# Multi-level attention with a four-layer feed-forward: softmax sums inverted and spread by DMAs, and a new order of tasks

## The reference

```
qkv = x @ w_in.T + b_in
scores = q @ k.T / sqrt(16);  attn = softmax(scores);  out = attn @ v
outs[l] = out @ w_out.T + b_out
```

## Time and profile before

| | us |
|---|---|
| median of 3 runs (lowest, highest) | 3565.03 (3562.65, 3567.78) |
| profiled execution, its own time | 3567.79 |
| profiled execution, span | 3566.0 |
| TensorE matmul busy | 3373.3 (95%) |
| VectorE busy | 2532.4 (71%) |
| ScalarE busy | 2529.9 (71%) |
| POOL busy | 1044.3 (29%) |

### The profile page before, as it was taken

The page is one execution under the profiler, slowest core; times in us unless marked ns, Lnnn a source line. Parts: engine busy times, 40 slices in busy tenths (PEclk is TensorE's granted clock), DMA queues, the critical chain, the costliest instruction groups (busy, mean ns, idle before and its releaser), DMA issues. The chain is left out here.

```text
span 3566.0 us, 58276 instructions
## 1 busy us (share of the span) xinstructions
PE 3373.3 (95%) x20635; PEld 1393.0 (39%) x20635; DVE 2532.4 (71%) x4805; ACT 2529.9 (71%) x3266; POOL 1044.3 (29%) x1060
## 2 busy tenths in 40 slices
PE   6999999999999999999999989799999999999998
PEld 3333333333333333333333322244444444444444
DVE  5989988988998998998998989634333333433333
ACT  2899889889889889889889878644444444444443
POOL 3343543544454454453464342300000000000000
PEclk7999999999999999999999999999999999999999
DMA  5343433433333333343343332200000000000000
GB/s 184 109 143 112 126 89 100 129 93 98 113 100 102 111 115 95 109 121 92 109 124 90 113 94 81 81 1 19 19 13 13 13 13 13 16 22 13 13 13 13
DMA packets 237691, 269.82 MB, mean 76 GB/s; under 512 B 55876, under 2 KB 203460, under 8 KB 236768
## 3 DMA queue, kind: packets, MB, share of 16 engines
q1 hardware_dynamic: 228144, 257.10, 24.2%
q10 hardware_dynamic: 9216, 8.39, 0.7%
HBM read 159.75 MB, written 101.45 MB: 73 GB/s over the span
## 5 line engine op out<-in xcount | busy, mean ns | idle before, releaser
L1009 ACT ACTIVATE a_probs<-a_p_s,a_unit_now 128x1024 f32<-128x1024 f32 x1360 | 1440.4, 1113 | 169.1 <-PE a_p_s L1407 164.9
L1135 DVE TENSOR_REDUCE a_part_max<-a_p_r 128x1 f32<-128x512 f32 x2048 | 1289.7, 679 | 112.9 <-PE a_p_r L1420 107.6
L1420 PE MATMUL a_p_r<-a_k_st,a_q_st 48*128 48x512 f16 (+2 forms) x2944 | 862.2, 374 | 94.1 <-DVE a_part_max L1135 44.3
L1757 PE MATMUL p_h<-f_h_hi,f_w_hi 128*128 128x512 f16 x2048 | 777.8, 380 | 9.8 <-issue 9.8
L1757 PE MATMUL p_h<-f_h_lo,f_w_hi 128*128 128x512 f16 x2048 | 777.6, 380 | 0.0
L1468 PE MATMUL a_p_o<-a_probs,a_v_aug 128*17 128x512 f32 (+2 forms) x5888 | 724.0, 571 | 1.0 <-ACT a_raw L1019 0.2
L1407 PE MATMUL a_p_s<-a_q_st,a_k_st 50*128 50x512 f16 (+2 forms) x2944 | 646.0, 368 | 18.4 <-ACT a_probs L1009 15.6
L1420 PEld LDWEIGHTS a_p_r<-a_k_st,a_q_st 48*128 48x128 f16 x2944 | 217.4, 94 | 976.7 <-DVE a_part_max L1135 654.8
L1656 ACT ACTIVATE f_h_f<-p_h,f_sc_now 128x512 f32<-128x512 f32 x256 | 175.9, 687 | 524.8 <-PE p_h L1757 524.8
L1135 DVE TENSOR_REDUCE a_row_max<-a_p_r 128x1 f32<-128x512 f32 (+2 forms) x672 | 417.9, 679 | 33.7 <-PE a_p_r L1420 32.5
L1607 POOL TENSOR_TENSOR f_rstd<-f_var_eps,f_minus_half 128x1 f32<-128x1 f32 x64 | 35.5, 555 | 1222.5 <-DVE f_var_eps L1720 1222.5
(11 more groups left out here) (170 smaller groups left out, 4454.4 us busy)
## 6 DMA issues: line engine op xcount, KB each, us to landing
qk_scratch<-a_qk_room SPq DMA_DIRECT2D x288, 128.0 KB
a_q_st<-qk_scratch SPq DMA_DIRECT2D x240, 96.0 KB, 2.4
a_w_lo<-wqkv_inner SPq DMA_DIRECT2D x30, 768.0 KB, 5.6
a_a_lo<-a_attn SPq DMA_DIRECT2D x448, 32.0 KB, 2.0
a_k_st<-qk_scratch SPq DMA_DIRECT2D x64, 192.0 KB, 3.6
a_o_lo<-wo_inner SPq DMA_DIRECT2D x24, 512.0 KB, 3.6
a_qk_room<-wf SPq DMA_DIRECT2D x23, 512.0 KB, 3.8
a_k_st<-qk_scratch SPq DMA_DIRECT2D x112, 96.0 KB, 2.3
```

The lines of the kernel that those rows point to most:

```text
L1009: act.activation(probs[:, s % 2, 2 * p:2 * p + 2, :], p_s[:, 2 * p:2 * p + 2, :], ACT.Exp, scale=unit_now[:, lvl:lvl + 1]).then_inc(exp_do ...
L1135: dve.reduce_max(out, src, AX.X).then_inc(max_read.sem, 1)
L1420: ins = pe.matmul(p_a[:, r * size:(r + 1) * size], q_st[rows_of(j, ROWS), query_at:query_at + 128], k_st[rows_of(j, ROWS), key_at:key_at + ...
L1757: ins = pe.matmul(out, a, c, start=first and n == 0, stop=last and n == len(terms) - 1)
```

## The change

The kinds `turn` and the old `spread` leave VectorE. Three new kinds of SP come in, each one DMA a unit:

- `sums`: the four rows of sums of `raw` (4 partitions of 512 values) go to a new tile `sums`, 128 x 16, 32 partitions for each row.
- `rows`: after VectorE has inverted `sums` into `rec`, this brings `rec` back over the four rows of sums in `raw`.
- `spread`: each of these rows is copied from `raw` over the 32 partitions of its head in the `attn` tile. It first waits until `rows` has landed and until the ring's slot is free.

`invert` on VectorE now waits for `sums` to have landed, and for the `rows` of the unit two before. POOL's `attn` waits for `spread` to have landed. The code of the new kinds (`hold()` and `held` count up a semaphore that nobody waits for, between two waits):

```diff
+                        elif kind == "sums":
+                            sp.wait_ge(raw_done.sem, raw_done.value(it, n + 1))
+                            hold()
+                            rec_done.wait(sp, it, max(n - 1, 0))
+                            hold()
+                            sp.dma_start(sums[:, n % 2, :], raw[HD:128:32, n % 2, :]).then_inc(sums_in[n % 2].sem, 16)
+                        elif kind == "rows":
+                            sp.wait_ge(rec_done.sem, rec_done.value(it, n + 1))
+                            hold()
+                            sp.dma_start(raw[HD:128:32, n % 2, :], rec[:, n % 2, :]).then_inc(rows_in[n % 2].sem, 16)
+                        elif kind == "spread":
+                            rows_in[n % 2].wait(sp, it, n // 2 + 1)
+                            hold()
+                            packed[n % RING].wait(sp, it, PACKED[n - RING] if n >= RING else 0)
+                            hold()
+                            sp.dma_start(attn[:, n % RING, :], raw[HD:128:32, n % 2, :].unsqueeze(1).broadcast_to((HG, 32, W))).then_inc(spread_in[n % 2].sem, 16)
...
-                            pool.wait_ge(spread_done.sem, spread_done.value(it, 2 * n + 2))
+                            spread_in[n % 2].wait(pool, it, n // 2 + 1)
...
-                            dve.transpose(attn[:, u % RING, cols], raw[:, u % 2, cols]).then_inc(turned_done.sem, 1)
...
-                            dve.reciprocal(rec[:, n % 2, :], attn[:, n % RING, :].rearrange("p (c r) -> p c r", r=32)[:, :, HD]).then_inc(rec_done.sem, 1)
...
-                            dve.transpose(attn[:, u % RING, cols], rec[:, u % 2, part * W // 64:(part + 1) * W // 64].unsqueeze(2).broadcast_to((128, W // 64, 32)))\
...
+                            sums_in[n % 2].wait(dve, it, n // 2 + 1)
+                            dve.sem_inc(held.sem, 1)
+                            rows_in[n % 2].wait(dve, it, n // 2)
+                            dve.sem_inc(held.sem, 1)
+                            dve.reciprocal(rec[:, n % 2, :], sums[:, n % 2, :]).then_inc(rec_done.sem, 1)
```

All tables of places are new: `AT`, `OPEN`, `FIRST`, `LAST`, `HEAD` and the shifts. The last two weight chunks of the feed-forward get kinds of their own (`w3load`, `w3hi`, `w3lo`, `w3check`) with the same work. Of the tables, those that the text speaks of:

```diff
-MAX_TURN, SCORE_TURN, VALUE_TURN = (0.04, 0.06, 0.4, 0.55), (0.46, 0.55), 2.07
+MAX_TURN, SCORE_TURN, VALUE_TURN = (0.28, 0.31, 0.46, 0.47), (0.5, 0.65), 2.31
...
-    "sp": {"proj": 2.2, "neg": 1.6, "attn": 1.8, "finish": 1, "keep": 0.5},
+    "sp": {"proj": 1.58, "neg": 0.08, "attn": 2.77, "finish": 6.47, "keep": 0.21, "fstore": 2, "fout": 1, "rows": 0.62, "fetch": -6.21, "stack": -0.64, "spread": 0.94, "sums": -0.8},
...
-    "raw": (3.24, 5.08, 9.27, 13.29, 16.87, 21.29, 21.71, 30.29, 38.14, 46.3, 54.29, 61.79, 70.45, 78.28, 84.87,),
+    "raw": (3.77, 5.3, 9.3, 13.51, 17.44, 21.31, 22.86, 31.01, 38.34, 46.14, 54.34, 62.3, 70.48, 78.55, 85.5,),
-    "invert": (5.49, 9.38, 12.5, 13.78, 18.68, 21.82, 25.82, 32.81, 40.07, 48.94, 57.9, 63.07, 71.05, 79.13, 86.75,),
+    "invert": (5.39, 7.56, 12.71, 14.5, 19.78, 23.35, 25.87, 36.19, 40.35, 49.31, 56.14, 63.79, 73.01, 79.5, 86,),
+    "rows": (3.7, 7.65, 10.82, 14.18, 18.06, 23.28, 25.13, 35.09, 40.04, 46.63, 55.7, 61.86, 72.02, 80.81, 83.42,),
+    "spread": (4.87, 7.55, 12.98, 15, 19.55, 24.06, 25.13, 35.57, 40.8, 49.03, 55.55, 63.72, 75.91, 80.53, 84.59,),
+    "sums": (3.6, 6.6, 9.81, 13.95, 17.08, 22.11, 22.6, 32.48, 40.71, 47.12, 52.41, 62.6, 72.47, 78.6, 84.78,),
+    "neg": (-8.19, -3.41, -2.84, 1.12, 5.81, 9.43, 10.07, 18.54, 27.44, 34.62, 41.49, 50.15, 57.56, 65.85, 73.4,),
```

More of the change, by code:

```diff
@@ new lines @@
+    "unit": (0.6,),
+    "v": (-53.98, -31.12, -28.9, -10.53, 0.6, 2.64, 18.63, 20.55,),
+    "wcut": (-54.32, -36.47, -14.52, -6.85,),
+    "wload": (-90.83, -43.55, -19.17, -13.34,),
+    "x": (-99.01, -33.96,),
+    "xcopy": (-11.84, -4.09, 1.61, 7.69, 9.75, 14.62, 63.23, 23.4,),
+    "xcut": (-55.4, -9.03,),
+}
+FIRST = {"acut": 2, "attn": 5, "invert": 5, "max": 132, "neg": 8, "proj": 15, "raw": 5, "rows": 5, "score": 42, "span": 4, "spanned": 4, "spread": 5,
+        "stack": 9, "sums": 5, "unit": 1, "v": 8, "value": 19, "wcut": 4, "wload": 4, "x": 2, "xcut": 2}
@@ L341 @@
+    "pool": {"raw": -5.09, "invert": 2.49, "spread": -12.52, "attn": 4.17, "acut": -1.36, "fetch": -6.83, "sum": -7.83, "out": 0.08, "stats": 1.03,
+        "gather": -21.93, "finish": -1.23, "sums": 2, "rows": 4.33},
+    "sp": {"raw": 8.82, "invert": -1.22, "spread": 4.03, "attn": 4.22, "acut": -13.38, "fetch": -8.3, "sum": -7.97, "out": -1.95, "stats": 1.85,
+        "gather": 8.87, "finish": 3.71, "sums": 3.46, "rows": 1.82},
 }
```

198 lines of the change are left out of this document (85 added, 113 removed).

## The result

The changed kernel takes 3828.0 us, median of four runs (3824.3 to 3831.6); the kernel before, on the same chips, 3566.4 us (3562.7 to 3568.9). The ratio is 1.073, with an interval of 95% from 1.072 to 1.074: 262 us slower. I had forecast 3495 us, with a range of 3415 to 3567. The change goes the wrong way, and none of my rivals had its size either: the slowest of them, C, stood at 3613 us.

A forecast was written before the change was run, and what follows sets the result against it. VectorE was taken to pace the coarse part, with three engines holding each other in the fine part. Freed transposes -87, turns +10 and last batch +5 gave -72 us, hence 3495 us; range 3415 to 3567.

The forecast's parts named there:

- C: Rival: SP's order holds the queue at `rows` and `spread`, so scores start late at each unit; 3613 us, chance 0.12.
- Part 3: Three new DMAs a unit on SP: room for their issues, bytes hidden; taken 0, ends 0 and +6 us a batch.
- Part 4: Longer chain from raw copy to product, some 8 us: +10 us over seven batch turns, +5 in the last batch.
- The paragraph on four engines: New DMAs use 4 engines; 256 KB takes an estimated 2.4 us plus the fixed part, making the sum 14 us later.
- Part 1: Four transposes a unit leave VectorE: 168 us freed, gain 63 in coarse parts plus 24 in fine, 87 us.
- Rival A: ScalarE and TensorE take over at once; first part gives 5 a batch, second nothing: 3545 us, chance 0.18.
- Part 2: VectorE's reciprocal reads a packed tile and gets two waits: no difference taken, waits 0 to +1 us a batch.
- Part 5: New places in the order, within steps and at the opening: taken 0, trusted to 20 us either way.
- The sum: -87 + 10 + 5 = -72 us off the profiled 3567.8; median near 3494, said 3495.
- signs of being wrong: Score weight loads waiting for DMAs, reductions waiting behind a reciprocal, ScalarE above 95%, or a fine part short as the coarse.

## Why the prediction was wrong, step by step

The 262 us come apart by differences between neighbouring kernels: -29 (the division left out, old order), -22 (all the new places at once), +72 (the chain with a quick source, product free of it), +191 (the slow source), +49 (the product has to wait). That is 311 - 51, with rounding. The order in which they are taken matters little where two are on record: the source is worth 197 us when the product waits and 191 when it doesn't, the product's wait 42 us with the fast source (3630.9 - 3588.5) and 49 with the slow one.

**Step that failed first: parts 3 and 4, the copy's duration and its bytes.** I priced each new DMA at the 2.0 us of the packing, and wrote of the 31 MB "hidden". The write back bore it out, 1.4 to 2.8 us to the next issue, and so did the gather in half of the cases in which it was waited for (1.5 to 2.2 us to the reciprocal), but it went up to 8.7. The third copy, 32 times as large, took 6.4 to 8.7 us, where I had put 2 to 4.5 as the sign of being right. A bare chain of 8 us was 12.1 (raw copy's end at 1316.16 to product at 1328.26). Worse than the length was what I hadn't a term for: a copy that holds a quarter of the DMA engines for 5.3 us at every unit makes its neighbours late and their issues long, and against a fast source that alone is 191 us, though nobody's product waits for it. I looked at the DMA share (35 to 38%) and found room; it rose only to 0.47 and 0.38 in the two parts. A mean share says nothing of what a 4 KB copy meets that leaves right behind a slow one. I had read the one wait for `neg` in the earlier trace rows, 1.2 us, as a sign against trouble; it says only that these copies landed in time while nothing slow stood beside them.

**The paragraph on four engines.** The Trainium skill (DMA: Bandwidth & Descriptors, Why a DMA increments its semaphore by 16 and not by 1) had the count right: the view shows a quarter of the engines busy. My estimate of 2.4 us for the bytes, which rests on Where 436 GB/s comes from in the same page of the Trainium skill, fits the source in device memory, where a quarter of the engines moved 100 GB/s. Out of four partitions they moved 49, and with 16 engines it got no better. So even with that estimate the sum would have been 14 us later and on the wrong side.

**Part 1, VectorE's gain.** Mis-sized: 87 us with ends 35 and 168, measured 28.7 with the reciprocals gone too, under my lower end. As a mean the coarse part gave 3.0 us a batch, not 9, and the fine one 0.5, not 3. The last fine part gave 5.7, and at its end I had expected nothing. The work that went was less than I took as well: VectorE's busy row fell by 134.7 us in the changed kernel, 0.28 us a transpose, where I had generalised 0.35 from one pair in the earlier trace rows and foretold 168. I read 96% busy as "bound by VectorE" and took nearly all of what was freed. Rival A had this side right (its -35 is the nearest figure), though not the time.

**Part 2, waits of the reciprocal.** Taken 0, ends 0 to +1 us a batch. VectorE waited 119.2 us in all, 15 a batch. Its place is behind the raw copy's in the order, but raw copies came late and the gather left later still, as at the turn above: the reciprocal's turn had been due 5.65 us, of which the gather's own flight is 2.2. What waits for what is right as I named it, and the wait of VectorE for maxima went from 107.6 to 313.6 us; how much of it goes by way of the reciprocal no run divides.

**Part 3, SyncE.** 0.65, 0.61 and 0.55 us of issue, as taken; but I had not asked what they do to the issues behind them, up to 2.1 us for one DMA of 4 KB where 0.6 is the longest with the fast source. SP's holds for the chain are real, but the kernel with fewer of them took 4020 us. Rival C said "slower, by late hand-overs", decided from 0.6 us a unit; it was 311 / 120 = 2.6. Its effect came, scores that wait for `neg`, and came mainly by the slow source, not by the holds that C named.

**Part 4, turns.** +1.5 us each, with ends 0 and 5. This turn went from 10.3 to 14.0 us; all seven went from 9.5 to 14.0 as a mean, +4.5 each or 31 us, inside the ends but three times the 10 that I took. The waits for POOL of 1.9 and 3.0 us at unit 0 are the 2 to 3 that I named. But the same wait, 2.1 us, stands at unit 6 within the batch, where I had said that 16 us are time enough; in all there are 23 such waits, 46.6 us. At the end of the last batch I took +5, with ends 0 and 8: from the last raw copy to the output matmul that needs it it was 10.4 us and is 26.1, +15.7. The copy is a part of that; another is that SP issues eight packings, 5.0 us, before it comes to the gather.

**Part 5, places.** Taken 0, trust 20: measured -21.6 without the chain, a little beyond what I trusted. With transposes in the same places it was +86, so the term has no one size.

**The sum.** 3567.8 - 72 = 3495.8, less the 2.8 of the profiled execution, is 3493; I wrote 3494 and said 3495. It changes nothing.

**A term that I hadn't: TensorE's clock.** The mean granted clock is 0.91 and 0.97 in the two parts, where it was 0.97 and 1.00: in the changed kernel, in which TensorE waits more, more of the time stands at 1.2 GHz in place of 2.4. Its row of matmuls is 70 us longer with the same matmuls. How much of the 262 us that is, no run shows; it is contained in the differences above.

Of what I had named as signs of being wrong, two came: scores that wait for DMAs, and waits at the reciprocal.

## What to carry to other kernels

Before a copy within the core's memory is called cheap, ask what it reads, and time that shape: 256 KB out of four partitions took 5.3 us on a quarter of the DMA engines and no less on all of them. A transfer that no product waits for still costs what it delays; look which small copies are issued behind it. To learn what an edit can bring at most, leave the whole step out first: that kernel gave 29 us where the busy rows had promised 87, or 0.24 us a unit as all that a replacement may cost.

## What the runs showed of the hardware

- A copy that reads four partitions (16, 48, 80 and 112) 32 times each moved 49 GB/s on a quarter of the 16 DMA engines, and no more (mostly 16 to 41) when all 16 were busy with it; a quarter of the engines moved 100 GB/s out of device memory. Other numbers of partitions were not tried.
- Such a copy costs as much from another queue: its source was worth 191 us in SyncE's queue and 193.5 us in ScalarE's, of which some 37 us were ScalarE's own waits.
- Two DMAs of 4 KB took up to 2.7 us to issue right behind it, 1.2 us right behind the same copy out of device memory, and 1.1 to 1.2 us in the kernel before.
